# Larger groups of edges, a spill tile and one-window visits in a graph kernel's gather and scatter passes

## The chip, the cores and the metric

The kernel runs on one NeuronCore of a Trainium2 chip. The metric is the device time of one execution in microseconds. TensorE (PE) does matrix products into PSUM, VectorE (DVE) and ScalarE (ACT) do elementwise work and reductions, GpSimd (POOL) here only issues indirect DMAs, and SyncE (SP) issues plain DMAs. Each engine has its own instruction stream, and they meet through semaphores. TensorE has two clock levels, 1.2 and 2.4 GHz; the profile gives the clock that was granted as a share of 2.4 GHz.

## The reference

Four graph layers run over one graph of 12,500 nodes with 64 features and 200,000 edges. `dst` is sorted and denser at low node numbers; `src` is random. The first two layers also read edge features. The last three aggregations (two SAGE layers and one GCN layer) are plain neighbour sums:

```python
src = jax.random.randint(jax.random.fold_in(_gk, 2), (200000,), 0, 12500, jnp.int32)
dst = jnp.minimum((12500 * jax.random.uniform(jax.random.fold_in(_gk, 3), (200000,)) ** 2.0).astype(jnp.int32), 99999)
...
msg = h[src]
agg = jax.ops.segment_sum(msg, dst, num_segments=n_nodes)
...
h_neigh = agg / jnp.maximum(deg, 1.0)
return h @ W_self + h_neigh @ W_neigh + b
```

Everything is float32. In the kernel a row of 64 features is kept as three bfloat16 parts (192 columns), whose sum gives the float32 value.

## The kernel before

Nodes lie in 98 windows of 128. The program runs, in order: a setup, an edge pass and the node work of layer 0, an edge pass of layer 1 (together to about 5,945 us), then `cells_setup()` and three times a `cell_pass()` with `prepare_table()` and `node_stage()` between them, one pass for each neighbour sum.

`cells_setup()` handles the edges in *groups* ("cells") of 1,408 edges (128 partitions by 11 tiles), 144 groups. For a group it ranks the edges within each source window (at most `CAP` = 32 of one window), and makes two things that the passes use again: a 0/1 matrix in fp8 of 32 columns for each window (which node of the window goes to which of its 32 slots), stored in DRAM, and the target of each slot. Its loop treats four groups in a turn. VectorE makes one-hots and ranks (L837 to L872), TensorE does the prefix sums and turns them into slots (L888 to L910).

`cell_pass()` has, for each group `g`:

- *gather* (L1231, TensorE): 98 matmuls, one for each window, with the fp8 matrix as 32 weight columns and the window's 192 columns of features moving. Four windows share one slot tile of 128 rows, so that the 98 windows fill 25 slot tiles, of which the last is half full.
- *evict* (L1111 to L1114, ScalarE): the slot tiles go from PSUM to SBUF as bfloat16, in chunks of 5 tiles, from two PSUM buffers in turn.
- *place and one-hots* (`build`, L1137 and L1141, VectorE): for the pair of windows that begins at the group's lowest target window, one subtraction, then 25 comparisons of 128 by 256.
- *add* (L1241, TensorE): 50 matmuls for a pair of windows (25 slot tiles by 2 windows) into one PSUM bank.
- *add up* (L1146, L1152, VectorE): a reduction of the three parts (128 by 384 to 128 by 128), and an add into `agg`.

TensorE's stream interleaves a chunk of the gather of group g+1 with a chunk of the adds of group g. VectorE builds the one-hots of group g+1 before it waits for the sum of group g. If a group's targets reach past the first pair of windows, both engines run a further *visit*: VectorE builds another set of one-hots, TensorE waits for it and does 50 more matmuls, VectorE adds up. The order on each engine is the program's own; a loop turn holds six groups written out, preceded by a load of the schedule words (L1034) and closed by a branch (L1060). At the end, a part that is skipped by a branch treats edges past the 32nd of a window (none in these inputs).

Of the kernel before, what the change touches and what calls it, by code (L numbers as in the profile page):

```python
# [47 lines left out]
CELL_TILES = 11  # L48
CELL_EDGES = P * CELL_TILES
CELL_STEP = 6  # L50
CELLS = -(-EDGES // CELL_EDGES // CELL_STEP) * CELL_STEP
HALF_CELLS = CELLS // 2
CAP = 32
SLOT_TILES = 25
PAGES = 4 * SLOT_TILES
PICK = 5
AT_SLOT = PAGES * CAP // 4
CELL_ROW = AT_SLOT + SLOT_TILES
# [7 lines left out]
assert CELLS * CELL_EDGES >= EDGES and HALF_CELLS <= P and CELLS % 4 == 0 and 4 * CAP == P and CELLS < GROUPS  # L66
assert SLOT_TILES % PICK == 0 and WINDOWS == PAGES - 2
# [3 lines left out]
def build(nc, a):  # L71

    ctx = ExitStack()
    with ctx:
# [7 lines left out]
        x = sb("x", [P, WINDOWS, D])  # L82
# [7 lines left out]
        arena = sb("arena", [P, ARENA])  # L90
# [23 lines left out]
        past_source = wide[:, split_words:split_words + CELLS * CELL_TILES]  # L114
        past_target = wide[:, split_words + CELLS * CELL_TILES:split_words + CELLS * CELL_TILES * 3 // 2].bitcast(I16)

# [33 lines left out]
        table = nc.dram_tensor("table", (P * WINDOWS, D), F32, kind="Internal").ap()  # L150
        cells_d = nc.dram_tensor("cells_d", (CELLS, P, CELL_ROW), F32, kind="Internal").ap()
        lows_d = nc.dram_tensor("lows_d", (CELLS, PAGES * CAP), BF16, kind="Internal").ap()
# [13 lines left out]
        shared = {}  # L166
# [170 lines left out]
        def prepare_table(norm, parts_of, stored):  # L337
# [11 lines left out]
            s_st, st0 = again("s_prepare_store", 32 if stored else 0)  # L349
            with nc.Block() as block:  # L350
# [53 lines left out]
                @block.sync  # L404
                def _(sp):
                    for b, w in enumerate(both):
                        if stored == "h":
                            if norm:
                                sp.wait_ge(s_dve, dve0 + n_begin + 4 + 2 * (b + 1))
                            sp.dma_start(table.rearrange("(p w) d -> p w d", p=P)[:, w, :], h[:, w, :]).then_inc(s_st, 16)  # L410
                    if stored:
                        sp.wait_ge(s_st, st0 + 32)
# [306 lines left out]
        def over_cells(eng, body, before=0, after=0, step=CELL_STEP):  # L719

            for g in range(-before, step):
                body(g // step, g % step)
            with eng.Fori(1, CELLS // step - 1) as it:
                for r in range(step):
                    body(it, r)
            for g in range(CELLS - step, CELLS + after):
# [6 lines left out]
        def cells_setup():  # L733
# [5 lines left out]

            step = 4  # L740
            s_load, s_const, s_wide, s_page = sem("s_c_load"), sem("s_c_const"), sem("s_c_wide"), sem("s_c_page")
            e = CELLS * CELL_TILES
            csrc, cdst, page, source = (wide[:, i * e:(i + 1) * e] for i in range(4))
            csrc, cdst = csrc.bitcast(I32), cdst.bitcast(I32)
            nat = wide[0:HALF_CELLS, 4 * e:4 * e + 2 * CELL_EDGES].bitcast(I32).rearrange("p (q e) -> p q e", q=2)
            agg_flat = agg[:, :, :].rearrange("p w d -> p (w d)")
            values = agg_flat[:, 0:e * 3 // 2].bitcast(BF16).rearrange("p (e v) -> p e v", v=3)
            scratch = agg_flat[:, e * 3 // 2:e * 3 // 2 + e].bitcast(I32)
            most = agg_flat[:, e * 3 // 2 + e:e * 3 // 2 + e + CELLS]
            low, high, twice, words = (agg_flat[0:HALF_CELLS, 4200 + 16 * i:4200 + 16 * i + n].bitcast(I32)  # L750
                                       for i, n in ((0, 2), (1, 2), (2, 2), (3, 2 * SCHED)))
            words = words.rearrange("p (q f) -> p q f", q=2)
            count = agg_flat[0:HALF_CELLS, 4264:4266]

            upper_b, ones_b = (turned[:, i, 0:P // 2].bitcast(BF16) for i in range(2))
# [10 lines left out]
            ranked = room(CELL_TILES * PAGES).rearrange("p (t w) -> p t w", w=PAGES)  # L766
            rank = room(CELL_TILES)
# [1002 lines left out]
```

## Time and profile before

| | |
|---|---|
| median of 3 runs | 11673.12 us (11669.65 to 11679.07) |
| profiled execution | 11675.45 us, of which the span of the trace is 11673.7 us |
| busy, share of the span | PE 6711.7 us (57%), DVE 6155.7 (53%), ACT 2917.5 (25%), POOL 3090.0 (26%) |
| clock granted to TensorE, mean | 0.717 |
| the three cell passes | 7254 to 8650, 8737 to 10131, 10262 to 11643 us |
| `cells_setup()` | 5945 to 7194 us |

A busy share is an average over stages with different limits, so the table is only a start: what a change in one stage is worth is read in that stage. The clock is 1.0 when 2.4 GHz were granted and 0.5 at 1.2 GHz; a value between is a mixture over time. "Idle before, releaser" is the idle time just ahead of an instruction and what ended it; "issue" means that the profile shows nothing that it waited for.

### The profile page before, as it was taken

The page shows a single profiled execution, that of the slowest core. Times are in us where ns is not written, and L with a number is a line of the kernel's source. Part 1 is how long each engine was busy: PE and PEld are TensorE (multiplying, and loading weights), DVE is VectorE, ACT ScalarE, POOL GpSimd, SP SyncE. Part 2 cuts the span into 40 slices and gives each one's busy share as a digit, 9 for nine tenths or more (in the row PEclk, how much of TensorE's full clock was granted, in tenths as well). Part 3 has the DMA queues.
Part 4 walks back from the last instruction along what each step waited for, and adds up shares of the span by engine and source line. Part 5 has one row for each costly group of instructions (what it writes and reads, how often), then busy time and mean ns, then how long its engine had stood idle before and what let it go on. Part 6 is the DMA issues. An engine that isn't in the chain of part 4 may idle for free. (4 is left out here: it accounts for less than half of the span.)

```text
span 11673.7 us, 312850 instructions
## 1 busy us (share of the span) xinstructions
PE 6711.7 (57%) x115490; PEld 5241.7 (45%) x115491; DVE 6155.7 (53%) x19853; ACT 2917.5 (25%) x4088; POOL 3090.0 (26%) x3175
## 2 busy tenths in 40 slices
PE   1332333333444444444456665888878888688886
PEld 1222222222333333333345554666666666566665
DVE  3333333344333333333378887666656666666666
ACT  1111111111111111111100001555435554355553
POOL 5666666642444444444400000000000000000000
PEclk9555555556555555555578777999879999789988
DMA  2122122211222222222224553111101111011111
GB/s 71 48 49 48 46 49 49 48 31 49 60 59 58 60 58 58 60 58 60 59 81 150 149 150 106 51 51 51 44 27 51 52 49 48 24 46 51 51 49 43
DMA packets 326510, 700.75 MB, mean 60 GB/s; under 512 B 90944, under 2 KB 116160, under 8 KB 324534
## 3 DMA queue, kind: packets, MB, share of 16 engines
q1 hardware_dynamic: 198166, 563.55, 15.7%
q0 software_dynamic: 100352, 102.96, 4.5%
q8 instruction: 882, 14.45, 0.5%
q10 hardware_dynamic: 26656, 16.06, 0.4%
q14 instruction: 454, 3.72, 0.1%
HBM read 601.25 MB, written 81.02 MB: 58 GB/s over the span
## 5 line engine op out<-in xcount | busy, mean ns | idle before, releaser
L529 POOL DMA_INDIRECT arena<-table,arena x3136 | 3082.3, 983 | 2559.3 <-DVE arena L662 1596.6
L682 PE MATMUL ps_all<-arena 128*128 128x65 bf16 (+1 forms) x18816 | 1462.2, 231 | 2814.5 <-issue 2518.4
L1241 PE MATMUL ps_all<-arena 128*128 128x192 bf16 x22650 | 2407.5, 256 | 191.0 <-DVE arena L1141 157.2
L682 PEld LDWEIGHTS ps_all<-arena 128*128 128x128 bf16 x18816 | 1082.4, 121 | 3139.0 <-issue 3126.5
L1141 DVE TENSOR_SCALAR arena<-lanes,arena 128x256 bf16<-128x256 bf16 x11325 | 2260.7, 281 | 68.3 <-DVE arena L1137 2.9
L1241 PEld LDWEIGHTS ps_all<-arena 128*128 128x128 bf16 x22650 | 1895.6, 101 | 588.9 <-issue 571.7
L1111 ACT CAST arena<-ps_all 128x960 bf16<-128x960 f32 x1728 | 1657.1, 959 | 1880.7 <-PE ps_all L1231 1880.7
L610 DVE TENSOR_TENSOR agg<-ps_all,agg 128x130 f32 (+1 forms) x392 | 114.0, 291 | 3222.8 <-remote 1852.8
L1231 PE MATMUL ps_all<-wide,arena 128*32 128x192 bf16 x42336 | 1365.7, 257 | 498.8 <-issue 436.4
L1231 PEld LDWEIGHTS ps_all<-wide,arena 128*32 128x32 fp8e4 x42336 | 838.8, 99 | 879.1 <-issue 878.3
L402 POOL MEMSET wide<- 128x384 bf16 x4 | 1.7, 418 | 4393.3 <-POOLq L1314 3142.5
L704 PE MATMUL ps_all<-wide,arena 128*128 x9408 | 538.9, 241 | 442.9 <-DVE arena L617 395.2
L704 PEld LDWEIGHTS ps_all<-wide,arena 128*128 128x128 bf16 x9408 | 505.8, 131 | 476.0 <-issue 475.9
L573 ACT ACTIVATE arena<-arena 128x512 bf16<-128x512 f32 x196 | 125.2, 639 | 2258.1 <-DVE arena L654 2258.1
L601 DVE TENSOR_SCALAR arena<-lanes,place_of 128x256 bf16<-128x256 bf16 x3136 | 657.0, 296 | 61.0 <-DVE place_of L597 30.6
L1146 DVE TENSOR_REDUCE turned<-ps_all 128x128 f32<-128x384 f32 x453 | 252.7, 558 | 691.3 <-PE ps_all L1241 651.5
L567 ACT CAST arena<-arena 128x512 bf16<-128x512 f32 x392 | 244.4, 623 | 990.9 <-issue 554.6
L894 PE MATMUL ps_all<-arena,turned 128*128 128x300 bf16 (+3 forms) x2880 | 481.7, 335 | 0.0
L1113 ACT CAST arena<-ps_all 128x768 bf16<-128x768 f32 x432 | 345.2, 799 | 208.9 <-PE ps_all L1231 208.9
L1137 DVE TENSOR_SCALAR arena<-arena,first 128x25 f32<-128x25 f32 x453 | 108.2, 239 | 539.6 <-issue 537.6
L894 PEld LDWEIGHTS ps_all<-arena,turned 128*128 128x128 bf16 x2880 | 309.1, 116 | 153.7 <-issue 55.9
L617 DVE TENSOR_SCALAR arena<-arena,node_id 128x1024 bf16<-128x1024 int32 x392 | 277.6, 750 | 148.4 <-issue 109.8
(202 smaller groups left out, 4699.3 us busy)
## 6 DMA issues: line engine op xcount, KB each, us to landing
arena<-cells_d SPq DMA_DIRECT2D x432, 412.5 KB, 3.4
arena<-lows_d SPq DMA_DIRECT2D x144, 800.0 KB, 5.2
arena<-in_dst_rows SPq DMA_DIRECT2D x196, 512.0 KB
cells_d<-arena SPq DMA_DIRECT2D x144, 412.5 KB, 5.6
arena<-in_edge_attr SPq DMA_DIRECT2D x196, 256.0 KB
arena<-table,arena POOLq DMA_INDIRECT x3136
wide<-attr_d SPq DMA_DIRECT2D x588, 48.0 KB
attr_d<-arena ACTq DMA_DIRECT2D x49, 192.0 KB
```

The source lines that it names most:

```text
L529: nc.gpsimd.indirect_dma_start(rows_f[:, g % SLOTS, j, :], None, table, bass.IndirectOffsetOnAxis(ap=src[:, g * TILES + j:g * TILES + j + ...
L601: last = nc.vector.tensor_scalar(onehots[:, k, j, :], lanes[:, :], place[:, j:j + 1], None, ALU.is_equal)
L617: nc.vector.tensor_scalar(onehot_t[b][:, :, :].rearrange("p j e -> p (j e)"), side_i[:, slot, :], node_id[:, bass.ds(w + b, 1)], None, ALU ...
L682: last = nc.tensor.matmul(ps_pair[r % 2][:, b * width:(b + 1) * width], onehot[r % 2][b][:, j, :], value[r][:, j, i, 0:width], start=(b == ...
L704: last = nc.tensor.matmul(ps_hid[:, r % 2, j * D:(j + 1) * D], onehot_t[b][:, j, :], split[:, bass.ds(w + b, 1), i, :].rearrange("p o d -> ...
L894: last = nc.tensor.matmul(ps_rank[k][:, first_t:last_t, 0:PAGES], ones_b, cells[:, t:t + 1, :].to_broadcast([P, last_t - first_t, PAGES]), ...
L1111: nc.scalar.copy(picked[r % 3][:, tiles, :], of).then_inc(s_evicted, 1)
L1113: nc.scalar.copy(picked[r % 3][:, c * PICK:SLOT_TILES - 1, :], of[:, 0:PICK - 1, :])
L1141: last = nc.vector.tensor_scalar(hot[k][:, q, :], lanes[:, :], place[at][:, q:q + 1], None, ALU.is_equal)
L1146: return nc.vector.tensor_reduce(sums, ps_pair[k].rearrange("p (b i d) -> p b d i", b=2, i=PARTS), AX.X, ALU.add)
L1231: last = nc.tensor.matmul(ps_pick[(r + 1 + c) % 2][j * CAP:(j + 1) * CAP, q, 0:PARTS * D], gather_hot[k][:, w * CAP:(w + 1) * CAP], split[ ...
L1241: last = nc.tensor.matmul(ps_pair[k][:, b * PARTS * D:(b + 1) * PARTS * D], hot[k][:, q, b * P:(b + 1) * P], rows[:, q, :], start=(q == 0 ...
```

## The change

- `CELL_TILES` goes from 11 to 21, so a group has 2,688 edges and there are 75 groups. Since up to 49 edges of a group now come from one source window, the edges past the 32nd of a window go to a 26th tile, the *spill tile* of 128 slots. Its rows are not gathered by matmul: `prepare_table()` also stores the bfloat16 parts in DRAM (`table_b`), and POOL fetches, for each group, 128 rows by an indirect DMA (75 in a pass). The spill rows of all groups lie where `x` was, so `x` is stored to DRAM before passes 1 and 3 (`keep`) and read back behind passes 2 and 3 (`bring`).
- A visit now is one window, not a pair: 26 matmuls (25 slot tiles and the spill tile) into one of four PSUM buffers, with the half of the 256-wide one-hots that belongs to it; VectorE reduces 128 by 192 to 128 by 64. Only the windows that a group really reaches are visited. For these inputs `dst` gives 15 groups that reach 1 window, 28 that reach 2, 27 that reach 3 and 5 that reach 4: 172 visits in a pass and 107 sets of one-hots, where before there were 151 pairs of windows, each with its set.
- VectorE's order in a step: if there is a third window, its one-hots; then it waits for the first visit's sum and adds it up; then the one-hots of group g+1; then the further visits' sums.
- Chunks of 4 tiles instead of 5 (seven chunks in a group, the last with 2 gather matmuls and 2 adds). The slots' targets stay in SBUF (`slot_dst`) instead of coming with the fp8 matrix.
- A loop turn of a pass holds two groups instead of six. The loop of `cells_setup()` still holds four, with more matmuls in each: 361 for a group (1 + 20, 20, 21 + 16 + 10, 21, 168 and 84) where there were 130.
- The part for edges past all slots stands in a block of its own behind each pass, and is skipped.

```diff
-CELL_TILES = 11
+CELL_TILES = 21
-CELL_STEP = 6
+CELL_STEP = 2
-PICK = 5
+PICK = 4
...
 def prepare_table(...)
+                    if keep:
+                        for w in both:
+                            sp.dma_start(x_d[:, w, :], x[:, w, :]).then_inc(s_kept, 16)
                     for b, w in enumerate(both):
+                        if stored == "parts":
+                            sp.wait_ge(s_dve, dve0 + n_norm + 3 + b)
+                            sp.dma_start(table_b.rearrange("(p w) n -> p w n", p=P)[:, w, :],
+                                         split[:, w, :, :].rearrange("p w i d -> p w (i d)")).then_inc(s_parts, 16)
...
 def cell_pass(...): TensorE
+            def segment(to, hot, half, rows, spill, tiles):
+                for q in tiles:
+                    last = nc.tensor.matmul(to, hot[:, q, half * P:(half + 1) * P],
+                                            rows[:, q, :] if q < SLOT_TILES else spill,
+                                            start=(q == 0), stop=True, skip_group_check=True)
+                return last
...
                                 if c == 0:
                                     hold(pe, s_hot, (g0 + (r + 1)) * 2)
-                                    hold(pe, s_done, g0 + (r + 2))
+                                    hold(pe, s_done, g0 + (r + 1))
+                                if c == n_pick - 1:
+                                    hold(pe, s_spilled, g0 + (r + 1))
...
-                        low, end, more = of[r]
+                        low, end, more, pairs = of[r]
+                        with pe.If(low + 1 < end):
+                            hold(pe, s_add_more, more + (low + 2))
+                            segment(ps_extra[0], pairs_hot[k], 1, picked[k], rows_of, every).then_inc(s_sum_more, 1)
                         with pe.If(low + 2 < end):
                             with pe.Fori(low + 2, end, 2) as w:
-                                hold(pe, s_hot_more, more + w)
-                                add(k, picked[r % 3], range(SLOT_TILES)).then_inc(s_sum_more, 2)
+                                hold(pe, s_hot_more, pairs + w)
...
 def cell_pass(...): POOL
+                    for g in range(CELLS):
+                        nc.gpsimd.indirect_dma_start(
+                            spill[:, g, :], None, table_b,
+                            bass.IndirectOffsetOnAxis(ap=spill_row[:, g:g + 1], axis=0)).then_inc(s_fetched[g % 4][0], 16)
...
 def cell_pass(...): VectorE, a step of a turn
                     def body(it, r, of):
                         g0 = it * CELL_STEP
+                        if there(it, r, 0):
+                            low, end, more, pairs = of[r]
+                            with dve.If(low + 2 < end):
+                                build(2, g, low + 2, s_place_more, pairs + (low + 2), s_hot_more)
+                        if there(it, r, 0):
+                            hold(dve, s_sum, g0 + (r + 1))
+                            add_up(ps_first[r % 2], low, (more + low) + g, s_done)
                         if there(it, r, 1):
-                            build((r + 1) % 2, (r + 1) % 2, cells[k], of[r + 1][0], s_place, (g0 + (r + 2)) * 2, s_hot)
+                            build(k, g0 + (r + 1), low1, s_place, g0 * 2 + (2 * r + 4), s_hot)
-                        hold(dve, s_sum, g0 + (r + 1))
-                        add_up(r % 2, (g0 + r) * 2 + (low + more - 1), low)
+                        with dve.If(low + 1 < end):
+                            hold(dve, s_sum_more, more + (low + 1))
+                            add_up(ps_extra[0], low + 1, (more + low) + (g0 + (r + 1)), s_add_more)
```

The first place is TensorE in a cell pass, before: the end of one group's step and its branch (L1231 gathers, L1241 adds, L1286 the test for a further visit).

```order
L1231 MATMUL ps_all<-wide,arena 32x192 x20
L1241 MATMUL ps_all<-arena 128x192 x10
L1231 MATMUL ps_all<-wide,arena 32x192 x18
L1241 MATMUL ps_all<-arena 128x192 x10
L1286 REGISTER_ALU
L1286 COMPARE_AND_BRANCH
L1287 UNCONDITIONAL_BRANCH
L1287 ISA
L1241 MATMUL ps_all<-arena 128x192 x50
L1287 REGISTER_ALU
L1287 COMPARE_AND_BRANCH
L1286 UNCONDITIONAL_BRANCH
```

The same place now (L1332 gathers, L1198 the adds of one window, L1359 the test for a second window, L1362 for a third).

```order
L1332 MATMUL ps_all<-wide,turned 32x192 x2
L171 REGISTER_ALU
L1198 MATMUL ps_all<-store 128x192
L1198 ISA
L1198 MATMUL ps_all<-store 128x192
L1359 REGISTER_ALU
L1359 COMPARE_AND_BRANCH
L171 ISA
L1198 MATMUL ps_all<-store 128x192 x26
L1359 UNCONDITIONAL_BRANCH
L1362 REGISTER_ALU
L1362 COMPARE_AND_BRANCH
```

The last chunk has shrunk to 2 gathers and 2 adds with the spill tile's wait between them, and a further window costs 26 matmuls in place of 50.

The second place is VectorE at the head of a loop turn, before: the schedule load, the one-hots of group g+1, then the wait for the sum of group g.

```order
L1034 TENSOR_LOAD sched
L163 ISA
L1137 ISA
L1137 TENSOR_SCALAR arena<-arena,first 128x25
L163 ISA
L1141 TENSOR_SCALAR arena<-lanes,arena 128x256 x25
L163 REGISTER_ALU
L163 ISA
L1146 TENSOR_REDUCE turned<-ps_all 128x128
L163 REGISTER_ALU
L1152 ISA
L1152 TENSOR_TENSOR agg<-turned,agg 128x2x64
```

And now (the first two rows are the conditional set for a third window; L1273 and L1277 are `build`, L1205 and L1210 the adding up).

```order
L1273 TENSOR_SCALAR turned<-wide,first 128x26
L171 REGISTER_ALU
L1277 TENSOR_SCALAR store<-lanes,turned 128x256 x26
L1294 UNCONDITIONAL_BRANCH
L171 ISA x2
L1205 TENSOR_REDUCE turned<-ps_all 128x64
L1210 ISA
L1210 TENSOR_TENSOR agg<-turned,agg 128x64
L1273 ISA
L1273 TENSOR_SCALAR turned<-wide,first 128x26
L171 ISA
L1277 TENSOR_SCALAR store<-lanes,turned 128x256 x26
```

The one-hots of the next group have moved behind the wait for this group's first sum.

## Rows read from the trace of the kernel before

**Rows 1.** of four stages: start:end, length, then busy us (instructions) by engine, clock
```profile
7254.00:8650.00 1396.00, 1179.40 (x21662) 913.23 (x21662) 921.93 (x4227) 697.36 (x864) 0.00 (x0) 0.90 0.16 47
...
10262.00:11643.00 1381.00, 1163.48 (x21662) 910.52 (x21662) 918.42 (x4227) 697.33 (x864) 0.00 (x0) 0.91 0.16 48
5945.00:7194.00 1249.00, 804.74 (x18732) 613.33 (x18732) 1094.45 (x1177) 44.29 (x288) 0.00 (x0) 0.79 0.49 145
2760.00:5900.00 3140.00, 1397.74 (x20474) 1130.21 (x20476) 1060.15 (x2953) 350.76 (x592) 1493.16 (x1564) 0.57 0.21 58
```

**Rows 2.** groups of instructions by line, whole span
```profile
L529 POOL DMA_INDIRECT arena<-table,arena x3136 | 3082.3, 983 | 2559.3 <-DVE arena L662 1596.6 <-issue 879.4 <-POOLq L350 83.3
L1241 PE MATMUL ps_all<-arena 128*128 128x192 bf16 x22650 | 2407.5, 256 | 191.0 <-DVE arena L1141 157.2 <-issue 8.5 <-ACT arena L1111 1.2
L1141 DVE TENSOR_SCALAR arena<-lanes,arena 128x256 bf16<-128x256 bf16 x11325 | 2260.7, 281 | 68.3 <-DVE arena L1137 2.9
...
L1231 PE MATMUL ps_all<-wide,arena 128*32 128x192 bf16 x42336 | 1365.7, 257 | 498.8 <-issue 436.4 <-DMA arena<-cells_d 32.6 <-ACT arena L1114 26.2
...
L1146 DVE TENSOR_REDUCE turned<-ps_all 128x128 f32<-128x384 f32 x453 | 252.7, 558 | 691.3 <-PE ps_all L1241 651.5 <-issue 39.8
```

**Rows 3.** timeline of a cell pass: start us, duration us, engine, line
```profile
7901.69 0.60 PE L1231 MATMUL ps_all<-wide,arena 128*32 128x192 bf16 x20
...
7902.22 1.01 PE L1241 MATMUL ps_all<-arena 128*128 128x192 bf16 x10
...
7903.16 0.59 PE L1231 MATMUL ps_all<-wide,arena 128*32 128x192 bf16 x18
...
7905.94 0.29 DVE L1152 TENSOR_TENSOR agg<-turned,agg 128x128 f32 x1 [0.24 <-DVE turned L1146]
...
7906.61 0.24 DVE L1137 TENSOR_SCALAR arena<-arena,first 128x25 f32<-128x25 f32 x1 [0.39 <-issue]
7907.00 4.99 DVE L1141 TENSOR_SCALAR arena<-lanes,arena 128x256 bf16<-128x256 bf16 x25
...
7911.50 1.01 PE L1241 MATMUL ps_all<-arena 128*128 128x192 bf16 x10
...
7912.94 0.56 DVE L1146 TENSOR_REDUCE turned<-ps_all 128x128 f32<-128x384 f32 x1 [0.95 <-PE ps_all L1241]
```

**Rows 4.** timeline just behind a turn of that loop
```profile
7921.62 0.99 PE L1231 MATMUL ps_all<-wide,arena 128*32 128x192 bf16 x20
...
7922.55 1.78 PE L1241 MATMUL ps_all<-arena 128*128 128x192 bf16 x10
...
7924.26 0.94 PE L1231 MATMUL ps_all<-wide,arena 128*32 128x192 bf16 x20
...
7929.52 0.56 DVE L1146 TENSOR_REDUCE turned<-ps_all 128x128 f32<-128x384 f32 x1 [4.19 <-PE ps_all L1241]
```

**Rows 5.** timeline, a second visit
```profile
8318.91 6.94 PE L1241 MATMUL ps_all<-arena 128*128 128x192 bf16 x50 [7.24 <-DVE arena L1141]
```

**Rows 6.** DMA queues in a cell pass, 7320 to 8640
```profile
q8 instruction: 268, 4.39, 1.4%
```

**Rows 7.** DMA queues in the set-up loop, 6050 to 7100 (its only row)
```profile
q1 hardware_dynamic: 50141, 157.26, 50.5%
```

**Rows 8.** closing branches and the schedule load on TensorE’s queue: ns min/median/max
```profile
L1060 PEldq COMPARE_BRANCH  x69: 77/4623/5202, 7310.7 to 11584.2; - x69
...
L723 PEldq COMPARE_BRANCH  x34: 83/215/225, 6040.4 to 7142.0; - x34
...
L1034 PEldq TENSOR_LOAD <-sched x72: 1872/1881/1900, 7259.0 to 11584.3; - x72
```

**Rows 9.** VectorE by line in the set-up loop, 6050 to 7100
```profile
L872 DVE TENSOR_SCALAR arena<-arena,next_id 128x3200 fp8e4<-128x3200 bf16 x126 | 236.6, 1877 | 0.0
L849 DVE TENSOR_REDUCE arena<-arena 128x11 f32<-128x1100 f32 x126 | 163.7, 1299 | 41.9 <-DVE arena L845 41.9
```

**Rows 10.** DMA issues, 2700 to 2900: KB each, us to landing
```profile
table<-h SPq DMA_DIRECT2D x2, 1568.0 KB, 6.9
```

More of the change, by code:

```diff
@@ L881, in body @@
                         g0 = it * step
+                        if within(it, r, 0, step):
+                            hold(pe, s_over, g0 + (r + 1))
+                            hold(pe, s_summed, g0 + (r + 1))
+                            now = over_cap[r % 2]
+                            to = ps_sums[:, at_over:at_over + CELL_TILES]
+                            last = nc.tensor.matmul(to, upper_b, now, start=True, stop=False, skip_group_check=True)
+                            for t in range(CELL_TILES - 1):
+                                last = nc.tensor.matmul(
+                                    to[:, t + 1:], ones_b, now[:, t:t + 1].to_broadcast([P, CELL_TILES - 1 - t]),
+                                    start=False, stop=True, skip_group_check=True)
+                            if not within(it, r, 1, step):
+                                last.then_inc(s_sums, 1)
@@ L882, in body @@
                         if within(it, r, 1, step):
-                            k, cells = (r + 1) % 2, cell_of[(r + 1) % 4]
+                            cells = cell_of[(r + 1) % 4]
                             hold(pe, s_cell, g0 + (r + 2))
-                            if within(it, r, -1, step):
-                                hold(pe, s_masked, g0 + r)
+                            for b in range(4):
+                                for t in range(b * BANK_TILES, (b + 1) * BANK_TILES):
+                                    last = nc.tensor.matmul(
+                                        ps_sums[:, b * PAGES:(b + 1) * PAGES], same_b, cells[:, t, :],
+                                        start=(t == 0 and not within(it, r, 0, step)), stop=True, skip_group_check=True)
@@ new lines, in body @@
+                                if t + 1 < end:
+                                    nc.tensor.matmul(rank_tiles(t + 1, end), ones_b,
+                                                     cells[:, t:t + 1, 0:WINDOWS].to_broadcast([P, end - t - 1, WINDOWS]),
+                                                     start=False, stop=True, skip_group_check=True)
+                            hold(pe, s_summed, g0 + (r + 2))
+                            before = sums[(r + 1) % 2]
+                            for b in range(4):
+                                for lo in range((b + 1) * BANK_TILES, CELL_TILES, BANK_TILES):
+                                    end = min(lo + BANK_TILES, CELL_TILES)
+                                    last = nc.tensor.matmul(
+                                        rank_tiles(lo, end), ones_b,
+                                        before[:, b * PAGES:b * PAGES + WINDOWS].unsqueeze(1).to_broadcast(
+                                            [P, end - lo, WINDOWS]), start=False, stop=True, skip_group_check=True)
@@ L1008, in room @@
+            s_fetched = [again(f"s_fetched{k}", 16 * len(range(k, CELLS, 4))) for k in range(4)]
+            at = [SPILL_WORDS - WINDOWS * D]
             def room(n):
@@ L1296, in _ @@
+            past_pass()
+            s_back, back = again("s_x_back", 32 if bring else 0)
+            with nc.Block() as block:
+                @block.sync
+                def _(sp):
+                    if bring:
+                        for b in range(2):
+                            w = slice(b * (WINDOWS // 2), (b + 1) * (WINDOWS // 2))
+                            sp.dma_start(x[:, w, :], x_d[:, w, :]).then_inc(s_back, 16)
                 @block.gpsimd
```

660 lines of the change are left out of this document (387 added, 273 removed).

## The prediction, written before the changed kernel ran

> **What bounds the kernel now.** I read the busy times of the stages first. The change touches only what runs from 5,945 us on: the set-up loop (1,249 us) and three cell passes of 1,396 to 1,381 us, about 1,390 each [rows 1]. In a pass TensorE is busy 84% of the time at a clock of 0.90, VectorE 66%, ScalarE 50%: TensorE carries it. In the set-up loop VectorE does, with 1,094 of 1,249 us.
>
> The lines of a pass then say what each visit costs: 22,650 adds on L1241 are 453 visits of 50 in three passes, 151 a pass; 11,325 one-hots on L1141 are 25 for each [rows 2]. The timeline gives the prices. A chunk of 20 gathers takes 7902.22 − 7901.69 = 0.53 us to the next chunk, a chunk of 10 adds 0.94 us [rows 3]. Behind a turn the same chunks take 0.93 and 1.71 us [rows 4]: that is the 1.2 GHz level. Two equations for each give 20 ns a gather and 77 ns an add at the high level, twice that at the low one, and a fixed 0.13 and 0.17 us a chunk for waits. Five pairs of chunks make 7.3 us a group. The turn is the other part: between reductions lie 7.8 us within a turn (7905.13, 0.81 before the add's start, to 7912.94), but 16.58 us across its end (7912.94 to 7929.52) [rows 3, 4]. So a turn costs some 9 us, 23 times a pass, 207 us.
>
> Why the turn is dear: the closing branch holds TensorE's queue for 4.6 us (median), while that of the set-up loop takes 0.2 us [rows 8]. In the passes queue q8 brings 4.39 MB of instructions to TensorE, 191 KB for each of 23 turns; in the set-up loop the DMA view has no instruction row at all [rows 6, 7]. The pass's turn holds 1,188 matmuls (6 × (98 + 50 + 50)), the set-up's 520 (4 × 130).
>
> **The change, part by part.** *Work in a pass.* Gathers fall from 144 × 98 to 75 × 98, adds from 151 × 50 = 7,550 to 172 × 26 = 4,472. At the high level: 75 × (98 × 0.020 + 7 × 0.13) = 215 us and 4,472 × 0.077 + 622 waits × 0.17 = 450 us (525 chunks and 97 extra windows). TensorE needs 665 us where it was busy 1,179. VectorE's one-hots fall from 151 × 25 to 107 × 26, at 4.99 / 25 = 0.200 us [rows 3] from 755 to 556 us. Neither is the pass's time, because the new order ties the two together.
>
> *The new chain.* The one-hots of group g+1 now start only after the first sum of group g, and TensorE can do one chunk of gather before it needs them. VectorE's link: 0.50 us from the last add (7911.50 + 0.94) to the reduction; 0.36 for the reduction (192 elements by the slope of L849, 1,299 ns for 1,100 elements, about 1.04 ns each and 0.15 [rows 9]); 0.24 to the add; 0.48 to the next instruction (before 0.67, with twice the elements and a test); 0.39 for the subtraction (7906.61 to 7907.00); 26 × 0.200 = 5.2. Sum 7.2, and 0.1 to TensorE. TensorE's link: a whole group is 26 × 0.077 + 7 × 0.17 + 98 × 0.020 + 7 × 0.13 = 6.06 us, less the first gather chunk 0.45, so 5.6 us high; low 4.0 + 1.2 + 3.9 + 0.9 less 0.8, so 9.3. A group of one or two windows thus takes 12.9 us high and 16.6 low. ScalarE's evictions, 697 / 144 = 4.8 us a group [rows 1] and a little more in smaller chunks, fit under both. The second window's 26 adds (2.3 us) lie in TensorE's idle part.
>
> *Which clock.* TensorE idles 7.3 us of such a chain less the extra windows. It was 0.57 where TensorE was busy 45% [rows 1] and 0.90 at 84%; here it is busy (6.1 + 1.3 × 2.3) / 14.7 = 62%, so about 0.72, half of the time low. One idle stretch of 7.24 us before L1241 made the next 50 adds take 6.94 us, 139 ns each [rows 5], nearly the low price throughout. I take the middle, 14.7 us. The Trainium skill (TensorE: Matmul & The Clock Gate, Part 1) says that the throttled state is the default and activity lifts it; by that alone every group would start low and could stay low, which is the second rival.
>
> *Three windows and more.* VectorE has two sets of one-hots (2 × 5.8), three adds-up (3 × 0.83), a wait of 0.5 and tests, some 15.3 to 15.6 us: it carries these. I take 15.6; for four windows 18.5, as the fourth waits for TensorE again. A pass: 43 × 14.7 + 27 × 15.6 + 5 × 18.5 + 14 for its start and end = 632 + 421 + 93 + 14 = 1,160 us. That is 230 less than 1,390, three times: −690.
>
> *The turn.* 37 turns instead of 23, but of 2 × (98 + 26 + 78) = 404 matmuls, below the 520 that ran without any fetch. So I price the branch at 0.2 us [rows 8] and the load of 12 words at less than the 1.88 us for 28. TensorE's part falls in its idle time, VectorE's (about 1.3 us) is hidden behind the next sum except with three windows. Bounds: 0, and the old 9 us (a rival).
>
> *Set-up.* VectorE per group before: 1,050 us / 126 = 8.33 us [rows 9]. Now 7,938 elements in 16 instructions at 1.04 ns and 0.15 us make 10.8, the fp8 matrix 3,136 × 1,877 / 3,200 = 1.84 us. There are some eight waits for its own results in place of three, at 0.33 us (41.9 / 126) each, against a slight overlap elsewhere: 1.6. Sum 14.3 us, × 75 = 1,073 against 144 × 8.33 = 1,200: −127. A few wide instructions more: +9. TensorE's turn here has 4 × 361 = 1,444 matmuls, more than the 1,188 that were fetched anew. TensorE has 5 us of slack in a group, so of 16 turns at 9 us I count 30 us; bounds 0 and 144. Together −88. The Trainium skill (Runtime: NRT & Kernel Launch, Instruction fetch mechanics) says that TensorE holds 2,048 instructions and that a taken branch outside them stalls for a fetch; with a weight load for each matmul 404 fit, 1,444 don't. By it the passes' turns are cheap and the set-up's are not, which is what the rows gave.
>
> *Around the passes.* `x` comes back in two DMAs; 1,568 KB landed in 6.9 us [rows 10], so both in some 13 us. Behind pass 3 about 10 us are exposed, behind pass 2 about 5. The stores of `x` and `table_b` lie beside the node stage, at most 10 us late in front of a pass. The skipped block is 4 us, three times. Sum +27. The 75 spill fetches at 983 ns on L529 [rows 2] are 74 us of a 1,160 us pass, and are issued ahead: nothing, unless the first is late by a few us.
>
> *Sum*, from the profiled span: 11,674 − 690 − 88 + 27 = 10,923. The execution was 2 us longer than its span and 2 us above the median shown, so 10,920 stands against 11,673.
>
> **The rivals.**
> 1. *The clock stays high.* Groups at 12.9, 15.2 and 17: 43 × 12.9 + 27 × 15.2 + 85 + 14 = 1,064 a pass, −978; 10,635 us. For it: within a turn the clock was high although chunks alternate. Against: idle parts of 5 to 7 us in most groups, and a low stretch behind each turn before [rows 4]. Chance 0.12.
> 2. *The clock stays low.* 43 × 16.6, 27 × 19.3 (TensorE then carries these: 10.1 + 2 × 4.3 + waits) and 5 × 23.8, + 14: 1,368 a pass, −66; 11,547 us. For it: the layer-1 edge pass at 0.57. Against: there TensorE was busy 45%, here it would be near 90% and regain the clock. Chance 0.07.
> 3. *The turns stay dear: slower than before.* If the code of a pass is still fetched at each turn, and now on both engines in the chain, 37 × 9.1 − 48 = 289 us a pass come on top: 10,920 + 867 = 11,787. It decides from 37 × 3 × t = 753, t = 6.8 us a turn more than I count. For it: more turns than before. Against: rows 6 to 8. Chance 0.04.
> 4. *Waits that I don't see* (tests with register values, POOL's order, set-up carried by TensorE at 16 us and its dear turns) cost 2 to 5 us a group: 11,250 to 11,500. Chance 0.09.
>
> **How the numbers follow.** My forecast of 10,920 has 0.68, and its own range is 10,720 to 11,180. With rivals 1 and 4 the range for 8 in 10 is 10,620 to 11,330. This kernel's runs differ by under 0.1%, so 0.2% (23 us) is about what can be told from no change. Only rival 3 and a worse form of 4 are slower: 0.05; within 0.2%: 0.01; faster: 0.94.
>
> **What would show it right or wrong.** Passes near 1,160 us; 22,050 gathers, 13,416 adds of one window, 8,346 one-hots (or 26 more in a pass by a branch). First sums some 14 to 15 us apart where groups reach one or two windows. TensorE idle before the first adds of a group with the one-hots as releaser, and not before anything else. Clock in the passes near 0.75. No q8 rows in the passes, but in the set-up loop. Set-up groups 14.3 us apart with VectorE nearly full. If the gap before the first adds is not the one-hots, or the branch at the turn takes microseconds again, the argument fails.

## The result, and the profile after

The changed kernel takes 11,269.48 us (median of 4, 11,259.8 to 11,291.52) against 11,671.39 for the kernel before on the same chip: a ratio of 0.966, 95% interval 0.9642 to 0.9678. That is 402 us less, where the forecast was about 750 less. The experiments below ran on four chips. On three of them the kernel before takes about 10,200 us, on the fourth 11,718. I call them the fast kind and the slow kind; the result above is from a chip of the slow kind (whether from that same fourth chip, the record doesn't say). Runs are compared only with runs of the kernel before on the same chip.

The stages of the profile after (start:end, length; busy us and instructions of PE, PEld, DVE, ACT, POOL; clock, DMA share, GB/s), which answer to [rows 1]:

```profile
5945.00:7160.00 1215.00, 811.23 (x27075) 689.47 (x27075) 939.31 (x1297) 67.40 (x301) 0.00 (x0) 0.75 0.27 78
...
7240.00:7347.00 107.00, 6.02 (x114) 3.69 (x114) 10.92 (x28) 4.92 (x7) 70.19 (x74) 0.50 0.22 42
7347.00:8544.00 1197.00, 811.08 (x11716) 564.49 (x11708) 665.77 (x3204) 370.00 (x518) 0.00 (x0) 0.82 0.09 26
...
8629.00:8736.00 107.00, 6.59 (x117) 4.05 (x118) 10.39 (x28) 5.10 (x8) 69.51 (x74) 0.50 0.22 42
8736.00:9864.00 1128.00, 786.36 (x11707) 547.51 (x11705) 664.64 (x3205) 369.72 (x518) 0.00 (x0) 0.83 0.09 26
...
10001.00:10113.00 112.00, 6.54 (x117) 4.00 (x118) 4.74 (x25) 5.12 (x8) 70.94 (x75) 0.50 0.25 53
10113.00:11235.00 1122.00, 779.62 (x11708) 543.04 (x11705) 664.88 (x3205) 370.28 (x518) 0.00 (x0) 0.84 0.09 26
```

Each pass begins with some 110 us in which every engine but POOL all but stands still (TensorE is busy for 6 to 7 us of them). Behind that it runs as forecast or a little faster (1,128 and 1,122 us), except that the first pass takes 1,197. The groups by line, 8,736 to 9,864 us (answering to [rows 2]), show who waits for whom in the body of a pass:

```profile
L1277 DVE TENSOR_SCALAR store<-lanes,turned 128x256 bf16<-128x256 bf16 x2756 | 549.6, 282 | 20.6 <-DVE turned L1273 18.0
L1198 PE MATMUL ps_all<-store 128*128 128x192 bf16 (+1 forms) x4471 | 542.5, 269 | 292.5 <-DVE store L1277 248.1 <-DVEq L1286 18.2 <-issue 14.9
...
L1205 DVE TENSOR_REDUCE turned<-ps_all 128x64 f32<-128x192 f32 x172 | 61.2, 356 | 439.8 <-PE ps_all L1198 428.2 <-DVE agg L1210 11.6
```

TensorE waits 248 us for the one-hots, VectorE 428 us for the sums: the two work in turn. The timeline of the second pass (answering to [rows 3, 4]) gives the lengths of the two links:

```profile
9105.88 0.80 PE L1198 MATMUL ps_all<-store 128*128 128x192 bf16 x4 [4.29 <-DVE store L1277]
9106.61 0.83 PE L1332 MATMUL ps_all<-wide,store 128*32 128x192 bf16 x16
...
9110.36 0.51 PE L1332 MATMUL ps_all<-wide,store 128*32 128x192 bf16 x16
9110.81 0.50 PE L1198 MATMUL ps_all<-store 128*128 128x192 bf16 x4
...
9120.32 0.80 PE L1198 MATMUL ps_all<-store 128*128 128x192 bf16 x4 [4.53 <-DVE store L1277]
```
```profile
9113.20 0.36 DVE L1205 TENSOR_REDUCE turned<-ps_all 128x64 f32<-128x192 f32 x1 [6.99 <-PE ps_all L1198]
9113.90 0.23 DVE L1210 TENSOR_TENSOR agg<-turned,agg 128x64 f32 x1 [0.34 <-DVE turned L1205]
9114.09 0.24 DVE L1273 TENSOR_SCALAR turned<-wide,first 128x26 f32 x1
9114.59 5.18 DVE L1277 TENSOR_SCALAR store<-lanes,turned 128x256 bf16<-128x256 bf16 x26 [0.26 <-DVE turned L1273]
```

VectorE's link is 9113.20 to 9120.32, 7.1 us; TensorE's is 9105.88 to 9113.20, 7.3 us, with the first chunks at the 1.2 GHz level (0.80 and 0.83 us) and the later ones at the 2.4 GHz level (0.50 and 0.51). Over the whole pass, first sums follow each other after 14.7 us in groups of one window, 14.8 in those of two, 15.2 with three and 17.9 with four.

Now the first 110 us. ScalarE, TensorE and POOL from 7,240 us on:

```profile
7245.65 0.80 ACT L1252 CAST store<-ps_all 128x768 bf16<-128x768 f32 x1 [2.14 <-PE ps_all L1332]
7262.64 0.80 ACT L1252 CAST store<-ps_all 128x768 bf16<-128x768 f32 x1 [16.20 <-issue]
7305.34 0.80 ACT L1252 CAST store<-ps_all 128x768 bf16<-128x768 f32 x1 [41.90 <-issue]
7343.84 1.50 ACT L1252 CAST store<-ps_all 128x768 bf16<-128x768 f32 x2 [37.70 <-remote]
```
```profile
7243.66 0.83 PE L1332 MATMUL ps_all<-wide,store 128*32 128x192 bf16 x16 [0.58 <-ACT store L1252]
7246.59 0.83 PE L1332 MATMUL ps_all<-wide,store 128*32 128x192 bf16 x16 [2.10 <-issue]
7263.59 0.83 PE L1332 MATMUL ps_all<-wide,store 128*32 128x192 bf16 x16 [16.16 <-issue]
7306.28 0.83 PE L1332 MATMUL ps_all<-wide,store 128*32 128x192 bf16 x15 [41.87 <-ACT store L1252]
```
```profile
7240.14 0.95 POOL L1224 DMA_INDIRECT store<-table_b,spill_row  x1 [0.30 <-issue]
7241.39 0.94 POOL L1224 DMA_INDIRECT store<-table_b,spill_row  x1 [0.30 <-issue]
```

TensorE's third chunk ends at 7243.66 + 0.83 = 7244.49, but ScalarE takes it at 7262.64, 18 us later; the chunk that ends at 7264.42 is taken at 7343.84, 79 us later. The trace's own records of semaphore updates agree: the signal of the second chunk, which ended at 7243.07, is recorded at 7245.54, and that of a late one at 7343.73, where the control below has each signal of its first chunks 0.01 to 0.03 us behind its chunk. In the other direction nothing is late: 0.15 us after ScalarE's end TensorE goes on. From 7,239 to 7,332.6 us POOL issues the 75 spill fetches in one row, one each 1.25 us; the last late signal comes 11 us behind the last of them. "Issue" and "remote" as releasers say that the profile saw no event that explains the wait.

### The profile page after: what moved, and what is told of

Its sections match the earlier page's. It is cut to its first block and busy times, and to the rows that moved or that the text cites. A ratio compares the mean times of both kernels' runs of the same rounds, so it can differ in the third digit from the quotient of the medians.

```text
span 11273.7 us, 261655 instructions
## 1 busy us (share of the span) xinstructions
PE 5642.4 (50%) x94327; PEld 4276.3 (38%) x94328; DVE 5264.0 (47%) x16996; ACT 1975.2 (18%) x3084; POOL 3317.6 (29%) x3400
## 5 line engine op out<-in xcount | busy, mean ns | idle before, releaser
L548 POOL DMA_INDIRECT store<-table,store x3136 | 3096.6, 987 | 2533.4 <-DVE store L681 1568.9
L701 PE MATMUL ps_all<-store 128*128 128x65 bf16 (+1 forms) x18816 | 1474.1, 232 | 2776.8 <-issue 2526.0
L701 PEld LDWEIGHTS ps_all<-store 128*128 128x128 bf16 x18816 | 1085.4, 122 | 3118.8 <-issue 3106.8
L1198 PE MATMUL ps_all<-store 128*128 128x192 bf16 x13416 | 1644.0, 270 | 925.9 <-DVE store L1277 793.8
L1277 DVE TENSOR_SCALAR store<-lanes,turned 128x256 bf16<-128x256 bf16 x8346 | 1666.0, 282 | 60.0 <-DVE turned L1273 46.1
L1198 PEld LDWEIGHTS ps_all<-store 128*128 128x128 bf16 x13416 | 1160.3, 105 | 1317.7 <-issue 1267.1
L1252 ACT CAST store<-ps_all 128x768 bf16<-128x768 f32 x1350 | 1078.2, 800 | 2620.5 <-PE ps_all L1332 2301.8
L1205 DVE TENSOR_REDUCE turned<-ps_all 128x64 f32<-128x192 f32 x516 | 183.5, 356 | 1338.5 <-PE ps_all L1198 1276.1
L723 PE MATMUL ps_all<-wide,store 128*128 x9408 | 537.5, 241 | 429.0 <-DVE store L636 389.4
L620 DVE TENSOR_SCALAR store<-lanes,place_of 128x256 bf16<-128x256 bf16 x3136 | 656.4, 296 | 61.0 <-DVE place_of L616 30.6
L723 PEld LDWEIGHTS ps_all<-wide,store 128*128 128x128 bf16 x9408 | 505.1, 130 | 460.1 <-issue 460.1
L1332 PE MATMUL ps_all<-wide,store 128*32 128x192 bf16 x11172 | 474.1, 296 | 353.0 <-ACT store L1252 204.0
L1332 PE MATMUL ps_all<-wide,turned 128*32 128x192 bf16 x10878 | 456.9, 294 | 128.4 <-issue 117.5
L1332 PEld LDWEIGHTS ps_all<-wide,store 128*32 128x32 fp8e4 x11172 | 256.9, 109 | 524.5 <-issue 522.8
L1332 PEld LDWEIGHTS ps_all<-wide,turned 128*32 128x32 fp8e4 x10878 | 249.6, 109 | 294.3 <-issue 293.0
```

The costliest lines, as they stand in the source:

```text
L548: nc.gpsimd.indirect_dma_start(rows_f[:, g % SLOTS, j, :], None, table, bass.IndirectOffsetOnAxis(ap=src[:, g * TILES + j:g * TILES + j + ...
L620: last = nc.vector.tensor_scalar(onehots[:, k, j, :], lanes[:, :], place[:, j:j + 1], None, ALU.is_equal)
L701: last = nc.tensor.matmul(ps_pair[r % 2][:, b * width:(b + 1) * width], onehot[r % 2][b][:, j, :], value[r][:, j, i, 0:width], start=(b == ...
L723: last = nc.tensor.matmul(ps_hid[:, r % 2, j * D:(j + 1) * D], onehot_t[b][:, j, :], split[:, bass.ds(w + b, 1), i, :].rearrange("p o d -> ...
L1198: last = nc.tensor.matmul(to, hot[:, q, half * P:(half + 1) * P], rows[:, q, :] if q < SLOT_TILES else spill, start=(q == 0), stop=True, s ...
L1205: return nc.vector.tensor_reduce(sums[:, 0:D], of.rearrange("p (i d) -> p d i", i=PARTS), AX.X, ALU.add)
```

## The experiments

All start from a control, the changed kernel with one register operation more at each wait on a loaded word (`ctl`), which keeps the number waited for at zero or above.

**The spill fetches and the start of a pass.**

```diff
 # pace
                     for g in range(CELLS):
+                        if g >= 4:
+                            pool.wait_ge(s_gathered, (g - 3) * n_pick)
                         nc.gpsimd.indirect_dma_start(spill[:, g, :], ...)
 # onefetch: only group 0's fetch is issued, and all groups read its rows
 # double: each fetch is issued a second time, into unused memory
```

> The changed kernel with one register operation more at each wait whose value comes from the loaded words (it holds the value at zero or above); the control for the experiments that follow. Some 250 such waits in a pass on each of VectorE and TensorE at 0.05 to 0.1 us, most of them in idle time: 11,260 to 11,300 us, and in each pass the same 95 to 115 us from its start to the first sum.

> POOL issues the fetch of group g only when group g-4 has been gathered, so about one fetch in 15 us in place of 75 in 93 us. Theory A (the unbroken row of fetches holds up TensorE's signals to ScalarE): the first sum comes 12 to 18 us after the start of a pass, in place of 107 to 119; three times 95 us go, 10,960 to 11,010 us. Theory B (the start of a pass is slow for a reason of its own: code that runs for the first time, the first matrices from memory): within 15 us of the control.

> Leaves out 74 of 75 spill fetches of a pass (all groups use the first one's rows, so the sums of the other groups are wrong by their spilled edges). Theory A: as the paced kernel, 10,950 to 11,010 us; if paced fetches still cost something each, it is faster than the paced kernel by 75 x 3 times that. Theory B: within 15 us of the control.

> Each spill fetch is issued twice, the second time into unused memory, so 150 back to back, some 187 us. Theory A: the first sum comes a further 93 us later in each pass, +280 us on the control, about 11,550. Theory B, or a fixed cost of the first fetches: within 30 us of the control.

These four came to a chip of the fast kind, where the kernel before takes 10,190 us. Ratios: control 0.9338 (0.9321 to 0.9355), paced 0.9337, one fetch 0.9312 (0.9297 to 0.9328), doubled 0.9332 (0.9313 to 0.935). The control's own absolute forecast missed, as it assumed the first chip. Neither theory of the stall could show itself, because here there is no stall: the control's ScalarE takes each chunk at once, with POOL issuing just as densely.

```profile
5744.06 1.50 ACT L1252 CAST store<-ps_all 128x768 bf16<-128x768 f32 x2 [8.54 <-PE ps_all L1332]
5745.97 1.50 ACT L1252 CAST store<-ps_all 128x768 bf16<-128x768 f32 x2 [0.41 <-PE ps_all L1332]
5747.88 1.50 ACT L1252 CAST store<-ps_all 128x768 bf16<-128x768 f32 x2 [0.41 <-PE ps_all L1332]
```
```profile
5741.50 0.94 POOL L1224 DMA_INDIRECT store<-table_b,spill_row  x1 [0.30 <-issue]
5742.75 0.94 POOL L1224 DMA_INDIRECT store<-table_b,spill_row  x1 [0.30 <-issue]
```

So the fetches cost almost nothing as such (0.3% at most, from `onefetch`), and what stalls belongs to the chip as well. The paced kernel on another chip of the fast kind repeated that:

> The kernel with paced spill fetches once more, since the first comparison ran on a chip on which the kernel before takes 10,190 us and the changed one shows no stall at the start of a pass (8 to 10 us to the first sum). Theory A1 (signals of TensorE come late while POOL issues fetches, on a chip where the kernel before takes some 11,670 us and on no other): if this chip is such a one, the first sum comes within 20 us of a pass's start and the ratio to the kernel before is 0.935 to 0.945, where the changed kernel's own was 0.966; if it is of the fast kind, 0.932 to 0.936 as before.

Ratio 0.9347 (0.933 to 0.9364). On a chip of the slow kind (before: 11,718 us) ran one kernel that paces the fetches (`six`) and one that doesn't (`set8`). They differ in loop sizes too, but the first group of a pass is written out ahead of the loop, so that the first 20 us run the same code; neither `pace` nor `ctl` itself ran on such a chip. From the first gather to the first sum:

| | pass 1 | pass 2 | pass 3 |
|---|---|---|---|
| changed kernel, first chip, slow kind | 113.4 us | 113.7 | 113.8 |
| `set8`, not paced, slow kind | 114.7 | 113.8 | 115.0 |
| `six`, paced, slow kind | 18.1 | 18.1 | 19.6 |
| `ctl`, not paced, fast kind | 18.3 | 18.0 | 16.1 |
| `double`, fast kind | 18.1 | 18.0 | 16.1 |

ScalarE at the start of the second pass, first in `set8`, then in `six`, and POOL in `six`:

```profile
8602.58 0.80 ACT L1252 CAST store<-ps_all 128x768 bf16<-128x768 f32 x1 [2.21 <-PE ps_all L1332]
8623.12 0.80 ACT L1252 CAST store<-ps_all 128x768 bf16<-128x768 f32 x1 [19.74 <-remote]
8667.22 0.80 ACT L1252 CAST store<-ps_all 128x768 bf16<-128x768 f32 x1 [43.30 <-remote]
8700.84 1.50 ACT L1252 CAST store<-ps_all 128x768 bf16<-128x768 f32 x2 [32.82 <-remote]
```
```profile
8542.10 0.80 ACT L1254 CAST store<-ps_all 128x768 bf16<-128x768 f32 x1 [8.55 <-PE ps_all L1334]
8543.68 1.50 ACT L1254 CAST store<-ps_all 128x768 bf16<-128x768 f32 x2 [0.78 <-PE ps_all L1334]
8545.59 1.50 ACT L1254 CAST store<-ps_all 128x768 bf16<-128x768 f32 x2 [0.41 <-PE ps_all L1334]
```
```profile
8541.99 0.94 POOL L1226 DMA_INDIRECT store<-table_b,spill_row  x1 [0.30 <-issue]
8547.85 0.97 POOL L1226 DMA_INDIRECT store<-table_b,spill_row  x1 [4.92 <-PE ps_all L1334]
8558.47 0.94 POOL L1226 DMA_INDIRECT store<-table_b,spill_row  x1 [9.65 <-PE ps_all L1334]
```

Theory A holds on that kind of chip: without the dense row of fetches the stall is gone, 95 to 97 us a pass. Theory B falls. Four fetches in a row do no harm there, 75 do. What in those chips makes the signals late was not found. Pacing spreads the issues and the transfers alike, so no run here tells which of the two does it, nor whether the recording of the profile has a part in it.

**VectorE's order in a step.**

```diff
 # early: the block of lines 1300 to 1303 stands ahead of lines 1296 to 1298
-                            hold(dve, s_sum, g0 + (r + 1))
-                            add_up(ps_first[r % 2], low, (more + low) + g, s_done)
                         if there(it, r, 1):
                             ...
                             build(k, g0 + (r + 1), low1, s_place, ..., s_hot)
+                            hold(dve, s_sum, g0 + (r + 1))
+                            add_up(ps_first[r % 2], low, (more + low) + g, s_done)
```

> VectorE makes the next group's one-hots ahead of its wait for the first sum, nothing else changed. Theory C (the forecast's chain: one-hots of VectorE, then adds of TensorE, in turn, 14.7 us a group): groups of one and two windows fall to the larger of VectorE's 7.5 us and TensorE's 6 to 8, say 8.5 us; those of three windows stay at 15.3 and of four at 18, so a pass takes 43 x 8.5 + 27 x 15.3 + 5 x 18 + 10 = 880 us in place of some 1,140, three times -260, about -780 us on the control. Theory D (the group's price comes from ScalarE's evictions, the waits of a chunk or code at the turns): less than 100 us.

Ratio 0.8808 (0.8793 to 0.8823), where the paced control beside it had 0.9347: 537 us less, of 780 that theory C expected. First sums are 8.4 to 8.7 us apart with one window (expected 8.5), 10.8 with two (expected 8.5, so this size was missed), 14.8 with three and 17.6 with four. The first two passes fall from 1,145 us to 929; the third took 1,104, by the next experiment's cause (it alone has the 185 fetches described there, and in `es` below, without them, it takes 925). Theory C holds, theory D falls: in the chain VectorE's one-hots lie end to end with TensorE's adds, and nothing else makes the 14.7 us.

**VectorE's loop and its code.** In the control one pass of three is slower, 1,208 us against 1,147. On the first chip, with slightly different code, it was the first pass, 1,303 us with its start against 1,234 and 1,228. That pass alone has 185 code fetches on queue q14, five for each of 37 turns (`ctl`, third pass):

```profile
q14 instruction: 185, 1.52, 0.5%
```

In that pass of the changed kernel VectorE stood 3.2 us (median) behind the turn's branch, in the second pass 0.24 us.

```diff
 # slot
+                if eng is nc.vector:
+                    eng.addr_align(256, offset=0, max_nops=0)
                 with eng.Fori(0, rounds) as it:
```

> VectorE's loop of a pass begins at the first instruction of a fetch block in each of the three passes, nothing else changed. Theory E (VectorE's loop lies over a block more in one of the three passes, which then fetches five pieces of 8 KB at each turn and pays some 4 us there): no pass has more than 10 pieces on queue q14, the pass of 1,200 us falls to 1,130, -70 us. Rival: the pieces belong to that pass's own code or data path: within 15 us of the control.

Ratio 0.9274 (0.9258 to 0.9289) against 0.9347 for `pace2` on the same chip, 68 us less. The third pass falls to 1,137 us, its queue to

```profile
q14 instruction: 5, 0.04, 0.0%
```

The Trainium skill (Runtime: NRT & Kernel Launch, Instruction fetch mechanics) gives engines other than TensorE room for 512 instructions, refilled in blocks of 16 KiB, and says that a taken branch whose target isn't in the current window of two pages waits for a fetch. That a loop's place then decides whether its head is still there is my inference. The trace agrees with a stall that hangs on the place (the same loop is 71 us cheaper in that pass when only its place changed), but not with the size of the blocks: 185 pieces made 1.52 MB, 8 KB each. The prediction took the same window for TensorE to be its 2,048 instructions, which the sentence on the branch doesn't say; the runs fit that reading, as turns of 404 matmuls and as many weight loads brought no code.

**Both together.**

```diff
 # es: early + slot;  esp: early + slot + pace
```

> The early one-hots and VectorE's loop at the start of a fetch block together. The early kernel's third pass ran at 14.7 us a group and its other two at 12.3: with the loop placed it should run at 12.3 too, 75 x 2.4 = 180 us less than the early kernel's 0.881, so a ratio of 0.860 to 0.866 on a chip of the fast kind. On a chip where the kernel before takes some 11,670 us, theory A1 adds 3 x 95 us at the starts of the passes: (11,270 - 3 x 215 - 70) / 11,670 = 0.904, and 107 to 119 us to the first sum.

> The same with paced spill fetches. On a chip of the fast kind: as without pacing, within 0.3%. On a slow one, theory A1: 285 us less than without, ratio 0.880, first sum within 20 us of the start of a pass; theory B (the starts are slow for a reason of their own there): as without pacing.

`es`: 8,820.68 us, ratio 0.8641 (0.8624 to 0.8658), as expected. `esp`: 8,821.91 us, 0.8646 (0.8629 to 0.8663), also as expected on a chip of the fast kind. All passes now take 925 to 933 us, and this version beats both kernels. Placing the loop is worth more here than in `slot`: the ratio falls from 0.8808 (`early`) to 0.8641, some 170 us, presumably because VectorE has less idle time left in which a fetch can hide; no run tests that. The third pass of `es`:

```profile
7860.00:8785.00 925.00, 733.26 (x11822) 520.34 (x11814) 667.52 (x3206) 374.98 (x525) 70.76 (x74) 0.91 0.13 36
```

It wasn't run on a chip of the slow kind. As an estimate from the stalls shown above, `esp` should be the better of the two there by some 285 us.

**What a turn costs.**

```diff
 # six (with the pacing of pace)
-CELL_STEP = 2
+CELL_STEP = 6
```

> Six groups to a turn of the pass instead of two (12 turns instead of 37; TensorE's turn then has 1,212 matmuls, VectorE's three times its code), with paced spill fetches, which changed nothing on a fast chip. Theory G (a turn is cheap only because its code stays on the engines): the closing branches take 3 to 5 us and queue q8 brings code at each turn, part of it in idle time, 4 to 12 us a turn, so 12 x 3 turns cost 145 to 430 us, less the 70 us that one pass already pays: ratio 0.940 to 0.970 where the control has 0.934. Rival (a turn costs about 1 us for its words and branches whatever its size): 75 turns less, ratio 0.926 to 0.932. On a slow chip theory A1 expects under 20 us from a pass's start to the first sum with the paced fetches.

Ratio 0.9422 (0.9404 to 0.9439). Theory G's range was given for a chip of the fast kind, and this is a slow one, where no paced control ran, so the ratio decides nothing; the groups below do. The rival falls: queue q8 brings code again and TensorE's closing branch takes 3.7 to 5.0 us (median by pass), where it takes 0.22 us with two groups to a turn. First pass of `six`:

```profile
q8 instruction: 148, 2.42, 0.9%
```

The groups are 15.36 to 15.52 us apart on average, where passes without fetches have 15.0 to 15.2 (`set8` on the same chip: 15.01 to 15.18). That is some 67 us over 36 turns, 2 us a turn. So a turn of long code is dear, as theory G says, but at half of its lowest price (4 us): most of TensorE's fetch lies in the time in which it waits for one-hots anyway. VectorE's turn is three times as long too and brings 101 to 111 pieces on q14 in each pass, so the 2 us are the price of both engines' code.

**The set-up's turn.**

```diff
 # hint
-            with eng.Fori(1, full - 1) as it:
+            with eng.bass.Fori(1, full - 1, ..., hint_back_edge=step == 4 and eng is nc.tensor) as it:
 # set8 (cell_of[r] becomes cell_of[r % 4], and one wait's count follows)
-            step = 4
+            step = 8
```

> TensorE's set-up loop tells its instruction fetch of the branch at its end ahead of time, nothing else changed. Theory F (the group across the turn takes 19.1 us in place of 14.3 because the closing branch fetches code, 3.3 us of it at the branch): 16 turns x 3.3 to 4.8 us go, -50 to -75 us. Rival (the turn is dear through VectorE's and the queues' state, or the fetched code comes no sooner): within 15 us.

> The set-up loop with eight groups to a turn instead of four, otherwise the control. Theory F2 (what the turn costs is the fetch at the closing branch, 4.2 us at each of 16 turns, and not code as such): 7 turns instead of 16, -38 us, ratio 0.930 where the control has 0.934. Rival (the missing time goes by groups, or a longer turn fetches as much within it): within 12 us of the control. On a slow chip, without pacing, 107 to 119 us from a pass's start to the first sum.

`hint`: 0.9345 (0.9329 to 0.936), no gain; the closing branch still took 3.6 us (median; 3.6 in `pace2` beside it, too), so this says only that the hint brought nothing, not what the branch costs. `set8`: groups within a turn stay at 14.5 to 14.6 us, the mean falls from 15.57 (changed kernel) to 15.16 us, 31 us over 75 groups where 38 were expected. The crossing of a turn became dearer (read at the reduction of line 914, 5.4 us over the other groups with four, 6.2 with eight), the number of turns fell from 16 to 7. Its ratio, 0.9573 (0.9555 to 0.9591) against 0.966, also holds that none of its passes has VectorE's fetches (105 in the whole program), worth some 70 us.

## Why the forecast was half right

The 11,269 us lie outside the forecast's own range (10,720 to 11,180), and inside the range for 8 in 10 (to 11,330) only by the end that rival 4 had widened. That rival priced unseen waits at 2 to 5 us in every group; what came was in the main one stall at the start of each pass, so that its range held is luck. On a chip of the fast kind the same change, as `ctl`, takes 680 us off (9,510.76 against 10,190.31).

*What bounds the kernel, and the new chain.* Right. The counts came as stated (22,050 gathers, 13,416 adds, 8,346 one-hots), TensorE waits ahead of a group's first adds for one-hots and hardly elsewhere, and 14.7, 15.6 and 18.5 us a group became 14.7, 15.2 and 17.9. `early` shows that the order is the cause. The clock in the bodies of the passes was 0.82 to 0.84 where I gave 0.75, but the middle between the two levels in TensorE's link was right. Without stall and fetches the passes take 1,303 − 95 − 68 = 1,140, 1,234 − 95 = 1,139 and 1,228 − 95 = 1,133 us against 1,160: 67 us in favour.

*The turn.* Right for TensorE: 0.22 us at the branch, 5 or 6 pieces of code on q8 in a whole pass, and `six` shows that a turn of 1,212 matmuls makes it dear. Not weighed was VectorE's own code. Whether its loop is fetched again at each turn hangs on its place in memory; in one of three passes it was, 68 us. The answer from which rows 6 were read has a row for it too, in the kernel before:

```profile
q14 instruction: 133, 1.09, 0.3%
```

*The spill fetches.* This step failed, a term put at nothing: "The 75 spill fetches at 983 ns [...] are issued ahead: nothing, unless the first is late by a few us". The price of the instructions was right and their data was in time, but on a chip of this kind, issuing them in one row holds up TensorE's signals to ScalarE. From the first gather to the first sum lie 113.6 us, and 18 to 20 when paced: 95 us a pass, 285 us in all. The rows for it were there before the change. In the edge passes, where POOL issues gathers, the profile of the kernel before lists a wait of VectorE that nothing explains (line, releaser: total us, times, longest us; 500 to 2,900 us):

```profile
DVE agg L610 <- remote: 874.5, 59, 23.8
```

The same wait in the changed kernel on the same chip, and what is left for that line in the control on a chip of the fast kind:

```profile
DVE agg L629 <- remote: 1000.3, 65, 23.8
```
```profile
DVE agg L629 <- PE ps_all L701: 3.2, 1, 3.2
```

The length of the wait is not yet how late the signal is. For the wait of 23.8 us that ends at 702.62, TensorE's last matmul for it ended at 690.38 and the signal is recorded at 702.28, 12 us later; by the same records the signals of that line's sums come up to 29 us late in the kernel before. The first half of the wait is TensorE itself, which there issues its matmuls one by one with pauses that nothing explains. Before, and in the control on the fast chip:

```profile
PE ps_all L682 <- issue: 1181.9, 1167, 4.4
```
```profile
PE ps_all L701 <- issue: 37.4, 17, 2.8
```

So on this kind of chip both TensorE's signals and its issuing suffer where POOL gathers. I read only the stages that the change touches, and the change moved POOL's work into one of them. It fits, too, that POOL's gathers end at 5,845 us on the first chip and at 4,388 in the control; that the whole difference of the chips comes from this was not tested.

*Set-up.* VectorE's group was right (14.3 us forecast, 14.5 measured within a turn at line 914). TensorE's turn was mis-sized: the group across it takes 19.9 us, 5.4 more, at 15 crossings 82 us, where I counted 30. That its code is fetched there came as forecast:

```profile
q8 instruction: 238, 3.90, 1.3%
```

The stretch from the first page one-hot to the first gather fell by 8 us (1,282 to 1,274) where I had −88 for it; the part of these 80 us that the turns don't explain, some 28, lies in the filling and emptying of the loop and in my price of the old groups, and was not separated.

*Around the passes.* +20 us between and behind the passes, where I had +27.

*Sum.* 285 (stalls) + 68 (VectorE's fetches) + 80 (set-up) − 7 (around) − 67 (groups) = 359 us over the forecast's 10,923. The span measured is 11,274, 351 over; 5 us of the rest lie ahead of the first page one-hot, where the changed kernel was that much earlier, and 3 in the rounding of the old passes. Without the stall and VectorE's fetches it would have taken about 10,920; that this is the forecast is in part luck, as a set-up 80 us too cheap stands against passes 67 us too dear. Rival 4 named the size and "POOL's order" but not this mechanism.

## What to carry to other kernels

Before moving an engine's work into a stage, look at what the others wait for wherever that engine does such work now: a wait with "remote" or "issue" beside a busy POOL can be a price that moves with POOL, as it was on one kind of chip here. Don't issue a long row of GpSimd's indirect DMAs because there is time; tie each to the progress of its user, which costs nothing where the row was harmless. And when two engines work in turn, ask first whether the one's next step really needs the other's last: here an exchange of two blocks, which needed no memory, was worth 537 us on a chip of the fast kind, where the whole change was worth 680, and some 720 together with the placing of one loop.

## What the runs showed of the hardware

- Chips differ by kind: the kernel before took 10,190 to 10,212 us on three chips, and 11,671 and 11,718 in the two sets of runs on the slow kind. There, signals of TensorE came up to some 80 us late at ScalarE and up to 29 us late at VectorE while GpSimd issued indirect DMAs one each 1.25 us; signals of ScalarE to TensorE didn't (0.15 us). With one such DMA a group, about each 15 us, the first sum of a pass came after 18 to 20 us, as on the fast kind. On the fast kind even 150 in a row did nothing.
- A branch hint at TensorE's closing branch brought nothing: 3.6 us with it and without.
